# A two-port step product, row statistics moved behind the x products, and a new order for the last round of the state-space layer

## The reference

```
y = ys.transpose(1, 0, 2, 3) + D[None, None, :, None] * xh
y = y.reshape(B, T, D_INNER)
y = y * jax.nn.silu(z)
y = y * jax.lax.rsqrt(jnp.mean(y * y, axis=-1, keepdims=True) + RMS_EPS) * norm_w
return jnp.einsum('bti,di->btd', y, W_out)
...
h = h + _L0_attn_ref(_layernorm(h, axis=-1), ...)
h = h + _L0_ffn_ref(_layernorm(h, axis=-1), ...)
```

## Time and profile before

| | |
|---|---|
| median of 3 runs | 1726.41 us (1725.41 to 1730.03) |
| the profiled execution | 1733.31 us, span 1731.6 us |
| granted TensorE clock, mean | 0.935 of full |
| busy: PE, DVE, ACT, POOL | 90%, 56%, 42%, 46% |
| layer, rounds 1 to 6 | 69.5 us a round |
| experts | from 1097 us to the end, 634 us |

### The profile page before, as it was taken

One profiled execution on the slowest core, in us unless ns is written; L12 is line 12 of the kernel. 1 busy time (PEld: TensorE's weight loads), 2 busy tenths in 40 slices (PEclk: granted clock), 3 DMA queues, 4 the chain that ended last, 5 costly groups with the idle time before them and its releaser, 6 DMA issues. The chain is left out here.

```text
span 1731.6 us, 31397 instructions
## 1 busy us (share of the span) xinstructions
PE 1558.0 (90%) x9263; PEld 1133.3 (65%) x9264; DVE 969.8 (56%) x2309; ACT 728.9 (42%) x1592; POOL 788.6 (46%) x678
## 2 busy tenths in 40 slices
PE   7999999987699999999999760499999999999997
PEld 7999999984566685775766430265565666565564
DVE  5555554532678989999999454143343434333343
ACT  2525343431856857858658100133333333333332
POOL 4330300011042247777777577455445555454554
PEclk9999999997889999999999575699999999999999
DMA  7210000003444443543532110477677777767665
GB/s 274 80 62 1 13 1 13 1 19 110 144 118 119 130 138 97 156 132 94 157 89 78 33 39 2 158 166 178 162 164 162 161 188 173 180 156 191 157 112 99
DMA packets 97702, 195.19 MB, mean 113 GB/s; under 512 B 38391, under 2 KB 46879, under 8 KB 92880
## 3 DMA queue, kind: packets, MB, share of 16 engines
q0 software_dynamic: 36992, 88.26, 23.4%
q1 hardware_dynamic: 60624, 105.78, 19.9%
HBM read 144.15 MB, written 49.84 MB: 112 GB/s over the span
## 5 line engine op out<-in xcount | busy, mean ns | idle before, releaser
L1902 PE MATMUL moe_ps_gu<-moe_wgu,moe_xt 128*128 x960 | 333.6, 491 | 0.0
L1760 POOL DMA_INDIRECT out_h<-moe_yy,moe_idx_s x121 | 190.8, 1577 | 260.3 <-DVE moe_idx_s L1822 111.0
L1028 POOL DMA_INDIRECT scratch_slots<-lay_toki,lay_slot x192 | 217.9, 1135 | 57.5 <-issue 57.5
L1902 PEld LDWEIGHTS moe_ps_gu<-moe_wgu,moe_xt 128*128 128x128 f32 x960 | 174.4, 192 | 97.0 <-issue 1.8
L1799 ACT ACTIVATE moe_sl<-moe_ps_gu 128x192 f32<-128x192 f32 x120 | 39.6, 330 | 365.0 <-PE moe_ps_gu L1902 365.0
L1299 PE MATMUL lay_ring<-head_wout,lay_yb 128*128 128x512 f32 x384 | 171.2, 600 | 0.0
L1431 DVE SCALAR_TENSOR_TENSOR lay_xa<-lay_ring,head_cw,lay_xa 128x378 f32<-128x378 f32 (+5 forms) x240 | 141.6, 609 | 51.4 <-ACT lay_xa L1086 45.5
L1215 PE MATMUL lay_ring<-lay_xnt,win_sb 128*128 128x128 f32 (+2 forms) x1152 | 163.3, 288 | 1.5 <-ACT lay_xnt L1118 0.7
L1754 POOL DMA_INDIRECT moe_xg<-scratch_xg,moe_idx_g x123 | 131.1, 1066 | 48.0 <-issue 23.9
L1215 PEld LDWEIGHTS lay_ring<-lay_xnt,win_sb 128*128 128x128 f32 (+2 forms) x1152 | 146.5, 195 | 6.9 <-issue 2.1
L247 POOL TENSOR_TENSOR tok_vv<-tok_w 128x512 f32<-128x512 f32 x16 | 16.6, 1038 | 261.4 <-ACT tok_w L449 227.1
(11 more groups left out here) (291 smaller groups left out, 2944.2 us busy)
## 6 DMA issues: line engine op xcount, KB each, us to landing
lay_m<-scratch_cum SPq DMA_DIRECT2D x16, 1536.0 KB
moe_wgu<-in_wgu SPq DMA_DIRECT2D x32, 768.0 KB, 5.7
moe_wd<-in_wd SPq DMA_DIRECT2D x32, 384.0 KB, 7.7
out_h<-lay_hres SPq DMA_DIRECT2D x48, 128.0 KB
scratch_xg<-lay_x SPq DMA_DIRECT2D x48, 128.0 KB
win_sb<-in_win SPq DMA_DIRECT2D x1, 4384.0 KB, 15.9
tok_u_raw<-in_tok_u SPq DMA_DIRECT2D x16, 256.0 KB, 4.4
tok_v_raw<-in_tok_v SPq DMA_DIRECT2D x16, 256.0 KB, 5.1
```

The source lines that it names most:

```text
L1028: pool.indirect_dma_start(out=a["slots"], out_offset=bass.IndirectOffsetOnAxis(ap=slot[i % 2][:, j, k:k + 1], axis=0), in_=toki[i % 2][:, ...
L1760: pool.indirect_dma_start(out=a["out"], out_offset=bass.IndirectOffsetOnAxis(ap=idx_s[n][:, 0:1], axis=0), in_=yy[n][:], in_offset=None, b ...
L1902: last = mm(ps_gu[b][:], xt[b][:, t], wgu[:, bass.ds(r * KD + t, 1)].rearrange("p o n -> p (o n)"), start=t == 0, stop=t == KD - 1)
```

## The change

Five edits, all in `build_layer` and `ring_order`. The step product (L1416) becomes a product of one tensor with a column, where it had a second tensor of ones. The row statistics of the three residual blocks leave `residual` and form `residual_stats`, behind the six `x_dt`; `routed_shift` goes behind the two convolutions. In round 7 the places of list 5 stand between the two halves of the state products (PE) and between the two halves of `skip` (DVE), and 8 of its scatters stand between the two gates on POOL. In round 7 `output(7, 0)` stands before the router's one-hot products, and the places of list 6 stand behind `output(7, 2)` and, on DVE, behind `routed_shift(7)`. The groups of POOL's list 5 in round 7 are 8, 3, 2, 8 and 3 DMAs, where they were 5, 4, 11 and 4.

```diff
         if 0 <= i - 2 < PAIRS - 2:
-            order.append(("pl", i - 2, 0))
+            order.insert(len(order) - (N_Y // 2 if i == PAIRS - 1 else 0), ("pl", i - 2, 0))
...
-            if j == 1 and i == PAIRS - 1:
+            if j == 2 and i == PAIRS - 1:
                 order.append(("pl", i - 1, 0))
...
-                    cuts = (0, 5, 12, 16, 3 * TOPK) if pairs(n) else (0, 5, 9, 20, 3 * TOPK)
+                    cuts = (0, 5, 12, 16, 3 * TOPK) if pairs(n) else (8, 11, 13, 21, 3 * TOPK)
                     if pairs(i):
                         gate_y(i, 0)
-                        gate_y(i, 1)
+                        if pairs(n):
+                            gate_y(i, 1)
                     if listed_late(w):
                         list_places(w)
                         count_marks(w)
+                        if not pairs(n):
+                            fill_lists(w, 0, cuts[0])
+                    if pairs(i) and not pairs(n):
+                        gate_y(i, 1)
...
+                    if listed_late(w) and not pairs(n):
+                        places(w)
                     for m2 in range(4):
...
-                    if listed_late(w):
+                    if listed_late(w) and pairs(n):
                         places(w)
+                    if pairs(i) and not pairs(n):
+                        output(i, 0)
...
-                    if pairs(i):
+                    if pairs(i) and pairs(n):
                         output(i, 0)
                         square_columns(i)
                         output(i, 1)
-                    if listed_early(r) and pairs(i):
-                        places(r)
+                    elif pairs(i):
+                        output(i, 1)
+                        square_columns(i)
                     if pairs(n + 1):
                         token_rows(n + 1)
                     if pairs(i):
                         output(i, 2)
+                    if listed_early(r) and pairs(i):
+                        places(r)
...
-                    own.step(v.scalar_tensor_tensor(dtr[:], td_in[32:48], ea[:], ones[0:NH].unsqueeze(1).to_broadcast([NH, 2, SEQ]),
-                                                    ALU.mult, ALU.mult))
+
+                    own.step(v.tensor_scalar(dtr[:], td_in[32:48], ea[:], None, ALU.mult))
...
-                    dve.wait_ge(res_done, i * 3 + j + 1)
-                    own.step(v.bn_stats(st[:], h[:, j]))
-                    own.step(v.bn_aggr(mv[:, j], st[:]))
-                    if j == 2:
-                        v.tensor_scalar(ve[:], mv[:, :, 1], EPS, None, ALU.add).then_inc(ve2_done, 1)
+
+                def residual_stats(i):
+                    h = hres[i % 2]
+                    for j in range(N_BLK):
+                        dve.wait_ge(res_done, i * 3 + j + 1)
+                        own.step(v.bn_stats(st[:], h[:, j]))
+                        own.step(v.bn_aggr(mv[:, j], st[:]))
+                    v.tensor_scalar(ve[:], mv[:, :, 1], EPS, None, ALU.add).then_inc(ve2_done, 1)
...
                     if pairs(n):
                         step_sums(n)
+                    elif listed_late(w):
+                        router_places(w)
...
-                    if listed_late(w):
+                    if listed_late(w) and pairs(n):
                         router_places(w)
...
                     for j in range(N_BLK):
                         if pairs(i):
                             residual(i, j)
-                        if listed_early(r) and j == 1:
-                            router_places(r)
                     for k in range(N_XT):
                         if pairs(n):
                             x_dt(n, k)
+
                     if pairs(i):
-                        routed_shift(i)
+                        residual_stats(i)
                     if pairs(n + 1):
                         conv(n + 1, 0)
                         conv(n + 1, 1)
+                    if pairs(i):
+                        routed_shift(i)
+                    if listed_early(r):
+                        router_places(r)
```

## The result

The changed kernel takes 1767.64 us (median of 6 runs, 1765.51 to 1771.65), the kernel before 1728.50 beside it (6 runs, 1725.41 to 1730.86). The ratio is 1.022, interval 1.020 to 1.024: slower by 39 us, where the forecast was 14 us faster. The profiled execution took 1767.17 us with a span of 1765.5, where before had 1731.6, and the mean granted TensorE clock fell from 0.935 to 0.908. The spans differ by 34 us only, because the profiled execution of before lies 4.8 us above the median of its six runs.

The account below looks back on a forecast made before the run. PE and DVE, nearly full, and a loop through both were taken to bound the middle rounds, POOL the last ones; 9.9+3.7 = 13.6 us off the median 1726.4 gave 1712.8, range 1706 to 1720.

Parts of the forecast that it names:

- What is late next: Middle rounds, from first residual r: statistics end at r+8.8, second gate at r+30.5, then 37.1 us; round taken as 67.7.
- middle rounds: Rounds up to 6: 3.7 us won in the first full round, 5.7 in four others, 0.5 before them; 9.9 us.
- DVE's own path: Middle rounds: statistics, convolutions, matrix and skips in sequence on DVE bring the last skip of sequence 0 at r+18.5.
- My bounds: Middle rounds gain 4.2 us at least, 14 to 17 at most; last rounds from nothing to 5.1.
- less 1 us that the half clock cost: Upper bound of middle rounds: PE's 66.7 us busy less this 1 us gives rounds of 66 to 67.
- the rivals: Stall goes to POOL 1718 us (0.2); step product escapes 1708 (0.08); last round loses 1735 (0.06); no tellable change 1722 (0.08).
- the rival on the other side: Round 7: router's weights over 4 us late delay `rr` and scatters; 1735 us at 12 late without middle gain; chance 0.06.
- last rounds: From round 6's first residual: list 6 begins at 79.4 us where it began at 83.1, a gain of 3.7.
- The list of what would show the forecast wrong: PE waiting over 1 us a round for silu or matrix, falling clock, late round 7 weights, experts off 634 by over 3.
- PE's waits at the x transposes: Rounds 1 to 6: waits of 15.5 us behind residuals and x products go near zero, 2.5 us each full round.
- The loop through POOL that the forecast built: Middle rounds: statistics hold `rstd`, scatters and both gates on POOL to r+30.5, then a 37.1 us chain; 67.6 a round.
- The step product: Beside POOL's gate it stays held; priced at nothing, alone saving some 0.2 us a round; rival that it escapes 0.08.

Follow-up runs that it names:

- e1_step: Kernel before with only the new step product: 1729.65 us beside 1730.77, ratio 1.0005.
- e5_fill: Changed kernel plus four unread 128x512 matrix products a round between the state products of sequences 0 and 1: 1723.87 us, ratio 0.995.
- e6_fill2: Changed kernel plus two unread 128x512 matrix products a round between the state products of sequences 0 and 1: 1716.79 us, ratio 0.993.

## Why the prediction was wrong

**The step that failed** is in "What is late next" of the middle rounds. It lists "DVE's own path (8.8, two convolutions 3.6, matrix 3.4, four skips 2.7)" and asks of it only when the last `skip` lets POOL go. It never asks when PE needs the matrix in the middle of that path. Its own numbers gave the answer: 8.8+3.6+1.7 = r+14.1 for the first half (measured r+13.9). PE's side was in the trace as well: in before the half came at r+16.4 and PE took it up at r+16.6 (824.08), a cover of 0.2 us. Free of its stalls and of the clock that fell with them PE is there at r+11.9. Stalls that are removed ahead of a wait with 0.2 us of cover (0.1 in the rounds at full clock) do not vanish, they move into it.

**The second error is larger in time: a wait was priced as its length.** The wait is 2.0 us, less than the 2.8 of idle time that PE had a round before, so by length the round would have been no longer than before. At full clock the products of a round take 65.5 us (`e1_step`, 327.72 in five rounds at 1.00); in the changed kernel they take 73.4. That is 7.9 us a round of clock, where before lost 1.2. (`e5_fill` gives 9.0: its 68.0 less 3.6 of fillers is 64.4 of products without a break, against 73.4.) My bounds had "less 1 us that the half clock cost" as the only term for the clock, with no upward side, so neither they nor the rivals held a loss in the middle rounds; the rival on the other side was put into the last rounds. The list of what would show the forecast wrong named both signs, the wait at the matrix and a clock that falls, but gave them neither a price nor a chance.

**What held.** PE's waits at the x transposes vanished. POOL waits 3.8 us for the statistics ahead of `rstd`, and its first gate starts at r+23.1 (forecast r+23.6); the second does not follow at once, since the state products at half clock bring the skips late:

```profile
767.76 0.88 POOL L1071 TENSOR_TENSOR lay_rstd<-lay_ve,head_mhalf 128x3 f32<-128x3 f32 x1 [3.80 <-DVE lay_ve L1502]
782.24 3.47 POOL L1001 TENSOR_TENSOR lay_yb<-lay_yb,lay_zs 128x1536 f32<-128x1536 f32 x1
789.67 3.44 POOL L1001 TENSOR_TENSOR lay_yb<-lay_yb,lay_zs 128x1536 f32<-128x1536 f32 x1 [3.96 <-DVE lay_yb L1456]
```

The loop through POOL that the forecast built is there when the clock stays up. Round 5 of `e6_fill2`, with zero at 800.12, shows it:

```profile
823.27 6.87 POOL L1001 TENSOR_TENSOR lay_yb<-lay_yb,lay_zs 128x1536 f32<-128x1536 f32 x2
830.16 2.45 ACT L1161 ACTIVATE lay_zs<-lay_ring 128x384 f32<-128x384 f32 x6 [2.60 <-POOL lay_yb L1001]
```

Both gates run back to back to r+30.0 (forecast r+30.5), ACT waits for their end, and the next residual comes 37.1 us later: 67.1, where the forecast had 67.6 and took 67.7. That the five rounds of `e5_fill` are 68.0 is no such confirmation. PE has no idle time in them, so its own work with the fillers sets them, and that they lie so near to 67.7 is luck.

The step product is held beside POOL's gate, as forecast, and is worth nothing here. In round 7 (zero at 985.16) the first gate starts at 21.6 (21.8 forecast), the second ends at 41.0 (41.5), `rr` at 63.8 (64.3), list 6 begins at 78.8 (79.4):

```profile
1006.78 3.44 POOL L1001 TENSOR_TENSOR lay_yb<-lay_yb,lay_zs 128x1536 f32<-128x1536 f32 x1
...
1022.69 3.45 POOL L1001 TENSOR_TENSOR lay_yb<-lay_yb,lay_zs 128x1536 f32<-128x1536 f32 x1
...
1048.08 0.88 POOL L1066 TENSOR_TENSOR lay_rr<-lay_ssv,head_mhalf 128x3 f32<-128x3 f32 x1 [9.31 <-DVE lay_ssv L1485]
...
1063.93 0.23 POOL L1014 TENSOR_TENSOR lay_slotf<-lay_posk,lay_hif 128x24 f32<-128x24 f32 x1
```

The gain is 4.3 us (3.7 forecast), and the experts take 634.9 us from the last scatter, 635.9 before.

**The sum by its terms:** middle rounds forecast -9.9, measured +38.8 (9.3 in the first, 29.5 in five); last rounds forecast -3.7, measured -4.3; start and experts 0, measured -0.5.

## What to carry to other kernels

When an edit lets an engine run ahead, follow it to its next wait on every producer, not only to the one that the edit makes late, and subtract the cover that each has now: here 0.2 us, when PE came 4.7 us earlier and the matrix only 2.5. A wait of TensorE is priced by what stands behind it: ahead of dense projections 2.9 us more cost 3.4, among small products with 64 columns of weights 10.8. If such a wait can't be scheduled away, a few useless dense products in it may be worth more than they cost, but measure them on more than one chip.

## What the runs showed of the hardware

Work that keeps PE busy does not by itself bring the clock back: after the wait it stayed at 0.50 for some 16 us of state products, transposes and logits with PE busy in all of them, and rose within the dense projections. It fell behind a stretch of such work with one idle time of 0.3 us in two rounds of `e6_fill2`, and with none in one round of before. A wait of 2.0 us among these products let it fall in every round, one of 0.9 us alone in none. And a chip can show idle times of PE, up to 2.3 us, that no semaphore ends, one of 0.4 to 0.8 us at 641 to 645 us among the z projections of six kernels, where the runs on the other chips show none in rounds 2 to 6; before was 7 to 12 us longer on those chips. Where they come from stays open.
